# Mixture-of-experts layer after attention: weight pieces at the middle of SyncE's round, job table in the loop's block, rows ahead of weights

## What is computed

```
mod = silu(c) @ wmod                          # sa, ca, ga, sb, cb, gb for each sequence
h = layernorm(x) * (1 + ca) + sa
Q, K, V = h @ Wq + bq, h @ Wk + bk, h @ Wv + bv          # 16 heads of 8
scores = Q K^T / sqrt(8) + Q . rel_table[clip(j - i + 64, 0, 128)]
x = x + ga * (softmax(scores) @ V @ Wo + bo)
h = layernorm(x) * (1 + cb) + sb
logits = silu(h @ rw1 + rb1) @ rw2 + rb2      # 8 experts, the best 2 per token, softmax of the 2
ffn = sum over the 2 chosen e: p_e * (silu(h @ w1[e] + b1[e]) @ w2[e] + b2[e])
out = x + gb * ffn
```

## Time and profile before

| | |
|---|---|
| runs, us | 953.19, 959.73, 956.13; median 956.13 |
| profiled execution, us | 956.31 |
| its span, first to last instruction, us | 954.5 |
| mean granted TensorE clock | 0.838 of 2.4 GHz |
| busy: PE, DVE, ACT, POOL | 68%, 60%, 61%, 56% |
| attention, from the span's start to the first instruction of the next block | 730.0 us |
| tables | to 742.5 us |
| experts | to 923.6 us |
| combine | to 954.5 us |

### The profile page before, as it was taken

One profiled execution on the slowest core, in us unless ns is written; L12 is line 12 of the kernel. 1 busy time (PEld: TensorE's weight loads), 2 busy tenths in 40 slices (PEclk: granted clock), 3 DMA queues, 4 the chain that ended last, 5 costly groups with the idle time before them and its releaser, 6 DMA issues. The chain is left out here.

```text
span 954.5 us, 18251 instructions
## 1 busy us (share of the span) xinstructions
PE 647.2 (68%) x4994; PEld 482.9 (51%) x4994; DVE 574.2 (60%) x2030; ACT 584.5 (61%) x1714; POOL 535.7 (56%) x821
## 2 busy tenths in 40 slices
PE   4678777877658585857658585857423499999900
PEld 3455555654436354534436354534213499899800
DVE  5878877765747584755747584754211166566517
ACT  2278887766647584846647584857101388888713
POOL 2545545848567484848567484836773045556534
PEclk9579999989788897979788897979665599999965
DMA  6766976581936547382836547391002588888627
GB/s 194 236 159 205 279 236 198 164 265 62 282 99 212 166 144 225 97 267 64 276 103 207 166 145 227 95 289 60 14 20 78 163 250 275 270 274 274 215 70 194
DMA packets 189433, 172.27 MB, mean 180 GB/s; under 512 B 18115, under 2 KB 175588, under 8 KB 189334
## 3 DMA queue, kind: packets, MB, share of 16 engines
q1 hardware_dynamic: 184070, 162.54, 55.8%
q0 software_dynamic: 4832, 8.44, 2.5%
q10 hardware_dynamic: 432, 0.14, 0.1%
HBM read 97.94 MB, written 74.63 MB: 181 GB/s over the span
## 5 line engine op out<-in xcount | busy, mean ns | idle before, releaser
L570 ACT ACTIVATE P<-NS,nmax 128x256 f32<-128x256 f32 x512 | 254.2, 499 | 162.9 <-DVE nmax L996 150.5
L947 DVE COPY stage<-psDist 128x768 f32<-128x768 f32 x125 | 119.3, 954 | 159.1 <-DMA dist_d<-stage 107.2
L996 DVE CUSTOM_DVE_ANT_0 NS<-psS,bias 128x256 f32<-128x256 f32 x512 | 185.5, 418 | 10.4 <-issue 8.4
L749 PE MATMUL psS<-Kst,Qst 32*128 32x256 f32 x512 | 69.5, 352 | 139.1 <-DVE nmax L996 138.9
L767 PE MATMUL psT<-ident,P 128*128 128x128 f32 x1024 | 147.6, 289 | 12.8 <-ACT PT L581 10.6
L581 ACT ACTIVATE PT<-psT 128x512 f32<-128x512 f32 x256 | 137.6, 582 | 20.8 <-PE psT L767 18.8
L767 PEld LDWEIGHTS psT<-ident,P 128*128 128x128 f32 x1024 | 126.0, 150 | 38.0 <-issue 25.9
L1349 POOL DMA_INDIRECT results_d<-y,row_u x87 | 86.1, 990 | 98.9 <-ACT y L1368 80.6
L749 PEld LDWEIGHTS psS<-Kst,Qst 32*128 32x128 f32 x512 | 41.6, 200 | 167.1 <-DVE nmax L996 156.3
L444 POOL TENSOR_TENSOR th<-z,th 128x512 f32<-128x512 f32 x32 | 40.7, 1273 | 145.9 <-ACT th L596 145.9
L570 ACT ACTIVATION_READ_ACCUMULATOR P<-NS,nmax 128x1 f32 x512 | 96.6, 189 | 0.0
(11 more groups left out here) (231 smaller groups left out, 1378.7 us busy)
## 6 DMA issues: line engine op xcount, KB each, us to landing
dist_d<-stage SPq DMA_DIRECT2D x128, 384.0 KB, 4.0
bias<-dist_d SPq DMA_DIRECT2D x256, 192.0 KB, 3.3
wUp<-pairs_d SPq DMA_DIRECT2D x29, 512.0 KB
wDown<-pairs_d SPq DMA_DIRECT2D x29, 512.0 KB
pairs_d<-pair SPq DMA_DIRECT2D x16, 512.0 KB, 3.1
x<-slots_d SPq DMA_DIRECT2D x29, 193.5 KB
raw<-in_L_ffn_w_dram SPq DMA_DIRECT2D x16, 256.0 KB, 3.7
y<-results_d SPq DMA_DIRECT2D x16, 256.0 KB, 4.9
```

Source lines behind the costliest of these rows:

```text
L570: act.activation(P[:, p % 2, h, q, :], NS[:, p % 2, h, q, :], ACT.Exp, scale=-1.0, bias=nmax[:, p % 2, k:k + 1], accum_out=lsum[:, b % 2, ...
L749: mm = pe.matmul(psS[:, h, S * q:S * q + S], Qst[at, b % 2, g, 128 * q:128 * q + 128], Kst[at, b % 2, g, :], start=True, stop=True)
L947: dve.tensor_copy(stage[:, p % STAGES, :, :, :], bank[:, :, 0:2 * RW].rearrange("p h (q c) -> p h q c", q=2)).then_inc(dist_out, 1)
L996: dve.tensor_tensor_reduce(NS[:, p % 2, h, q, :], psS[:, h, S * q:S * q + S], bias[:, p, h, q, :], 1.0, 3e38, ALU.add, ALU.min, nmax[:, p ...
```

## The change

It does four things.

1. **Weight pieces.** `store_piece(b - 1)` and `load_piece(b)` stand ahead of `write(b, 4)` instead of ahead of `write(b, 0)`.
2. **Job table and padding.** The work of `tables`, but for the gates, is put at the end of the streams of `attention`'s block. POOL makes the constants (three `iota`, two `memset`) in its opening part, PE's one matmul goes to `psM`, DVE's chain follows its last step, SP writes the fixed padding and that of experts 0 to 3, and ACT, through its own DMA queue, that of experts 4 to 7. The block `tables` is gone, and with it one meeting of all engines.
3. **Gates.** They are made in `combine`: PE's transpose and 16 products, ACT's copies between its exponential and its first scaling.
4. **Order of the first loads in experts.** SP waits for the rows and the padding first, then loads x of job 0, wUp of job 0, x of job 1, wDown of job 0, wUp and wDown of job 1.

The diff, without the declarations of tiles and semaphores and the calls:

```diff
@@ attention, SyncE
             for b in range(B):
-                if b > 0:
-                    store_piece(b - 1)
-                load_piece(b)
                 for n in range(PAIRS):
+                    if n == 4:
+                        if b > 0:
+                            store_piece(b - 1)
+                        load_piece(b)
                     write(b, n)
...
             sp.wait_ge(pair_out, 16 * B)
+            sp.wait_ge(consts_done, 1)
+            sp.dma_start(slots_d[UNUSED:UNUSED + ET, :].rearrange("(p k) e -> p k e", p=128),
+                         fill[:]).then_inc(filled, 16)
+            pad(sp, range(EXP // 2))
@@ attention
+        def pad(engine, experts):
+            engine.wait_ge(table, 1)
+            for x in experts:
+                n = engine.value_load(cnt_u[0:1, x:x + 1], min_val=0, max_val=TOKENS)
+                engine.dma_start(slots_d[bass.ds(n + AREA * x, ET), :].rearrange("(p k) e -> p k e", p=128),
+                                 fill[:]).then_inc(filled, 16)
@@ attention, GpSimd
-            then(pool.iota(token[:], [[TOKENS, 2], [128, TT]], base=0, channel_multiplier=1,
-                           allow_small_or_imprecise_dtypes=True))
+            pool.iota(steps[:], [[0, EXP], [ET, MOST]], base=0, channel_multiplier=0,
+                      allow_small_or_imprecise_dtypes=True)
+            pool.iota(until[:], [[1, EXP], [-1, EXP]], base=0, channel_multiplier=0,
+                      allow_small_or_imprecise_dtypes=True)
+            pool.iota(jobno[:], [[1, JOBS]], base=0, channel_multiplier=0,
+                      allow_small_or_imprecise_dtypes=True)
+            pool.memset(fill[:, :, 0:E], 0.0)
+            pool.memset(fill[:, :, E:ROW], float(NO_ROW))
+            pool.iota(token[:], [[TOKENS, 2], [128, TT]], base=0, channel_multiplier=1,
+                      allow_small_or_imprecise_dtypes=True).then_inc(consts_done, 1)
+            pool.wait_ge(consts_done, 1)
@@ attention, ScalarE, after its last step
+            pad(act, range(EXP // 2, EXP))
@@ attention, TensorE, after its last step
+            pe.wait_ge(totalled, 1)
+            pe.matmul(psM[:, 0:EXP], ones[:], total[:], start=True, stop=True).then_inc(counted, 1)
@@ attention, VectorE, after its last step
+            dve.wait_ge(keyed, 4 * B)
+            dve.tensor_tensor(total[:], earlier[:, TT, :], earlier[:, 0, :], ALU.subtract).then_inc(totalled, 1)
+            dve.tensor_tensor(p2[:], v2[:], v1[:], ALU.subtract)
...
+            dve.wait_ge(counted, 1)
+            dve.tensor_copy(cnt_u[:], psM[:, 0:EXP]).then_inc(table, 1)
+            then(dve.tensor_copy(cnt[:], psM[:, 0:EXP]))
...
+            dve.tensor_copy(expert[:], ex[:])
+            dve.tensor_copy(firstrow[:], first_f[:])
@@ mixture
-        tables(nc, ident, modT, v1, v2, earlier, ones, slots_d, p2, gbB, firstrow, expert, fill, filled)
@@ experts, SyncE
-            for j in range(2):
-                load_w(j, 0, wUp, up, 0, up_in)
-            load_w(0, 1, wDown, down, 0, down_in)
             for k in range(RINGS):
                 sp.wait_ge(sent[k], 16 * 4 * B // RINGS)
             sp.wait_ge(filled, 16 * (EXP + 1))
-            for j in range(2):
-                load_x(j)
-            load_w(1, 1, wDown, down, 0, down_in)
+            load_x(0)
+            load_w(0, 0, wUp, up, 0, up_in)
+            load_x(1)
+            load_w(0, 1, wDown, down, 0, down_in)
+            for n, w, arrived in ((0, wUp, up_in), (1, wDown, down_in)):
+                load_w(1, n, w, up, 0, arrived)
@@ combine, ScalarE
             act.activation(p2[:], p2[:], ACT.Exp).then_inc(probs, 1)
+            act.wait_ge(gates_turned, 1)
+            act.activation(gbR[:], psL[0:B, 0:E], ACT.Copy).then_inc(gates_out, 1)
+            for g in range(B * E // 512):
+                act.wait_ge(gate_rows, g + 1)
+                act.activation(gbB[:, 4 * g:4 * g + 4, :].rearrange("p b e -> p (b e)"),
+                               psG[:, g % 2, :], ACT.Copy).then_inc(gates_wide, 1)
             act.wait_ge(probs, 4)
@@ combine, TensorE
+            pe.transpose(psL[0:B, 0:E], modT[:, 5, :], ident[:]).then_inc(gates_turned, 1)
+            pe.wait_ge(gates_out, 1)
+            for g in range(B * E // 512):
+                past(pe, gates_wide, g - 1)
+                for k in range(4):
+                    b = 4 * g + k
+                    mm = pe.matmul(psG[:, g % 2, 128 * k:128 * k + 128],
+                                   ident[0:B, b:b + 1].broadcast_to([B, 128]), gbR[:],
+                                   start=True, stop=True)
+                mm.then_inc(gate_rows, 1)
@@ combine, VectorE
                 dve.wait_ge(summed, c + 1)
+                dve.wait_ge(gates_wide, c // 2 + 1)
```

More of the change, by code:

```diff
@@ L136, in program @@
                   ahead, rw1_s, rb1T, rw2_s, rb2T, w1, w2, pairs_d, rows, slot_u, v1, v2, earlier,
-                  ones, slots_d, sent)
-        mixture(nc, X, ident, modT, pairs_d, b1T, b2T, out_v, v1, v2, earlier, ones, slots_d, sent)
+                  ones, slots_d, sent, p2, firstrow, expert, fill, filled)
+        mixture(nc, X, ident, modT, pairs_d, b1T, b2T, out_v, slots_d, sent, p2, firstrow, expert, filled)
 def past(engine, semaphore, count):
@@ L249, in attention @@
         lower = t("lower", [128, 128])
+        steps = t("steps", [128, EXP, MOST])
+        until = t("until", [128, EXP, EXP])
+        total = t("total", [128, EXP])
+        cnt = t("cnt", [128, EXP])
+        cnt_u = t("cnt_u", [128, EXP], U32)
+        more = t("more", [128, EXP, MOST])
+        wide = t("wide", [128, EXP, EXP])
+        ntile = t("ntile", [128, EXP])
+        cum = t("cum", [128, EXP])
+        jobno = t("jobno", [128, JOBS])
+        gone = t("gone", [128, JOBS, EXP])
+        gone_t = t("gone_t", [128, JOBS, EXP])
+        ex = t("ex", [128, JOBS])
+        first_f = t("first_f", [128, JOBS])
         def pt(name, shape):
@@ L290, in attention @@
             sm("picked"), sm("keyed"), sm("slot_link"), sm("slotted"), sm("moved"))
+        consts_done, totalled, counted, table = sm("consts_done"), sm("totalled"), sm("counted"), sm("table")
         written = [sm(f"written{s}") for s in range(SLOTS)]
@@ L1120, in newton, with mixture @@
     then(dve.tensor_tensor(r, r, tmp, ALU.mult))
-def mixture(nc, X, ident, modT, pairs_d, b1T, b2T, out_v, v1, v2, earlier, ones, slots_d, sent):
+def mixture(nc, X, ident, modT, pairs_d, b1T, b2T, out_v, slots_d, sent, p2, firstrow, expert, filled):
     with ExitStack() as ctx:
@@ L1268, in experts @@
+        combine(nc, X, ident, modT, results_d, p1, p2, y_sent, out_v)
 def experts(nc, ident, slots_d, results_d, pairs_d, b1T, b2T, firstrow, expert, y, row_u, sent,
@@ L1484, in _, with combine @@
                         split_f(j, k)
-def combine(nc, X, results_d, p1, p2, gbB, y_sent, out_v):
+def combine(nc, X, ident, modT, results_d, p1, p2, y_sent, out_v):
     with ExitStack() as ctx:
@@ L1497, in combine @@
         y2 = t("y2", [128, TT, E])
+        gbR = t("gbR", [B, E])
+        gbB = t("gbB", [128, B, E])
+        psG = ctx.enter_context(nc.psum_tensor("psG", [128, 2, 512], FP))
+        psL = ctx.enter_context(nc.psum_tensor("psL", [128, 512], FP))
         loaded = [sm(f"loaded{c}") for c in range(CHUNKS)]
@@ L1529, in _ @@
                 i.then_inc(weighted, 1)
+        @block.tensor
+        def _(pe):
+            pe.transpose(psL[0:B, 0:E], modT[:, 5, :], ident[:]).then_inc(gates_turned, 1)
[8 more added lines that the diff above has]
+                mm.then_inc(gate_rows, 1)
         @block.vector
```

135 lines of the change are left out of this document (24 added, 111 removed).

## The result

The changed kernel takes 813.55 us (median of 4 runs, 812.11 to 816.34) against 956.36 us (median of 4 runs, 953.19 to 959.73) for the kernel before: a ratio of 0.851, 95% interval 0.8473 to 0.8547. The prediction was 844 us with a range of 824 to 872.

A forecast was written before the change was run, and what follows sets the result against it. The prediction took the kernel to be bound by DVE's copy waiting for stage writes held behind SP's store and POOL's split. 954.5 - 101.0 - 11.8 - 5.1 + 5.3 = 841.9, plus 1.8 outside the span, gave 844 us, range 824 to 872.

The forecast's parts named there:

- The convoy of store, write and copy: Attention's rounds: POOL's split holds SP's store, then the stage write, then DVE's copy, which waits 107.5 us in total.
- Part 1, the chain of the round: Attention's rounds: without the stall a round takes 33.3 us instead of 42.3, a gain of 101.0 us.
- The floor: Attention's rounds: POOL's list from mix to ready, 31.7 us, is the fastest round, adding 18 us to the gain.
- The moved wait: SP's store, now mid-round: still waits some 5 us a round for POOL's split, without delaying the copy.
- The cover of 7.8 us: Attention's rounds: the held write lands by 369.2, and the copy needing it comes at 377, 7.8 us later.
- Part 2, table and padding: End of attention: table and padding hide beside POOL's sends, so experts' first DMA leaves 11.8 us earlier.
- Part 4, rows first: Start of experts: loading x first brings the first up product 5.0 us after the first DMA, gaining 5.1 us.
- Part 3, gates: Combine: nothing covers the gates there, so the stage ends 5.3 us later.
- The second limit: Rival in attention's rounds: POOL falls half a step behind, rounds take 36.1 us, 875 us in all; chance 0.17.
- the hold that comes back: Rival in attention's rounds: SP's mid-round stop lets the ring run dry, rounds stay 42.3 us, 945 us; chance 0.04.
- the disturbance of DVE's copy by POOL: Slower rival in attention's rounds: POOL operations hold DVE, rounds take 53.9 us, 1119 us in all; chance 0.02.
- POOL's floor: Rival in attention's rounds: restarts after stalls cost more than thought, rounds go to 31.7 us, 826 us; chance 0.09.

The follow-up runs named there:

- the read first: The kernel before with the bias read of tile 7 put ahead of the store of the weight piece: 944.64 us, ratio 0.986.
- the keys go first: The changed kernel with GpSimd's keys for the second choice put ahead of its normalising of the next input: 808.16 us, ratio 0.8433.
- the run with tile 6: The changed kernel with the store and load of the weight pieces ahead of tile 6 instead of tile 4: 814.34 us, ratio 0.8505.
- at tile 2: The changed kernel with the store and load of the weight pieces ahead of tile 2 instead of tile 4: 837.56 us, ratio 0.8743.
- they go to the tail: The changed kernel with the gates made at the end of attention's block, behind the job table, instead of in combine: 808.38 us, ratio 0.845.

## Why the prediction was right or wrong

**What bounds the kernel: right.** The convoy of store, write and copy was the wait to remove, and it went, with the wait of 107.5 us down to 0.4.

**Part 1, the chain of the round: wrong in its size, and the cause of the miss.** "I follow a round without the stall" gave 33.3 us and put 0.6 us a round against the gain; the round became 31.4. The step that failed is the one that took two lengths from a round with the stall in it: "from the start of that copy to the next mix is 6.0 us" measured 5.4 (311.96 to 317.32), and the 19.3 us from mix to kmax measured 17.7 (317.32 to 335.04):

```profile
335.04 0.17 DVE L1066 TENSOR_REDUCE kmax<-key 128x2 f32<-128x16 f32 x1 [1.17 <-POOL key L496]
```

Both stretches lie right behind the gap. The first held about 0.7 us of waiting for the bias of tile 7, which stood behind the same store: with the read first it was 5.35 us. The second held TensorE at a granted clock of 0.50, since it had just stood still: with 88 transposes it was 17.7 us. These two runs made the round 0.9 and 1.9 us shorter. Steps 7 and 0 had lost 1.4 and 2.0 us; steps 1 and 6 gave 0.7 and 0.9 back when the gap went, which leaves 1.8 us a round beyond the idle time. Over the rounds the term was 101.0 us forecast and 128.6 measured (107.1 of idle time gone and 21.5 beyond it, where the prediction had taken 6.5 off). That is nearly the whole miss: the time is 30 us below the forecast, 27.6 of them here.

**The floor was no floor.** "There is no faster floor than POOL's list from mix to ready, 31.7 us" counted 1.5 us of POOL's own waits for DVE as work. With them gone POOL does its list in 31.4 us with 1.32 us of idling in it, and 30.6 us when the keys go first. So the low end of the range, built on this floor, was too high.

**The moved wait: right.** The store still waits in ten rounds and costs nothing; the run with tile 6 shows it. The cover of 7.8 us was the right kind of reckoning: at tile 2 it is overdrawn, by the write and by a bias, and the round is 1.8 us longer.

**Part 2, table and padding: right.** 11.8 us forecast, 11.3 measured. The table was done 2.5 us before the last send.

**Part 4, rows first: right.** 5.1 forecast; 5.2 measured to the first product (10.12 less 4.96) and 5.5 over the stage. The wUp load was the later of the two, as forecast: TensorE waited 1.62 us for it.

**Part 3, gates: right.** 5.3 forecast, 5.4 measured, and 5.2 come back when they go to the tail.

**Rivals.** The second limit and the hold that comes back did not happen, and neither did the disturbance of DVE's copy by POOL: it still takes at most 960 ns. POOL's floor, at 0.09, was the side on which the truth lay, and I had it right in one part ("the restart after each stall costs more than I think") without asking the trace for it. The granted clock was in the earlier trace rows as 0.88 for the round, and the prediction even said that it would rise, but put no time on it.

## What to carry to other kernels

When a stall is cut out of a loop, don't read the lengths of the steps behind it as their natural lengths. Take these from a round or a step that has no stall before it, and look at the granted clock of just those steps. A queue that works in order holds everything behind a wait: list all that stands there, not only the item whose wait has a name. A wait for a slow producer costs nothing at a place from which the next user is further away than the producer is late, and moving it further back than that gains nothing more.

## What was not expected of the hardware

Filling TensorE's idle gap with 88 useless transposes made the kernel 16 us faster (ratio 0.9832), while 52, behind which TensorE stood still for 4.5 us before the next scores, gave nothing (1.0015). In the one case the next pair of score products took 0.39 us at a granted clock of 1.00 and in the other 0.58 at 0.50.
